# Attention scores on TensorE: from four column strips with a stacked contraction of 97 rows to four row strips of 32, issued pair by pair

## What is computed

```python
N, S, D = x.shape                       # 4, 2048, 512
q = (x @ Wq.T).reshape(N, S, H, hd).transpose(0, 2, 1, 3)    # H = 16, hd = 32
k = (x @ Wk.T).reshape(N, S, H, hd).transpose(0, 2, 1, 3)
v = (x @ Wv.T).reshape(N, S, H, hd).transpose(0, 2, 1, 3)
energy = jnp.einsum('nhqd,nhkd->nhqk', q, k)
attn = jax.nn.softmax(energy / jnp.sqrt(jnp.float32(hd)), axis=3)
out = jnp.einsum('nhql,nhld->nhqd', attn, v)
...
x = _layernorm(x + _L0_attn_ref(x, L0_attn_Wq, L0_attn_Wk, L0_attn_Wv), axis=-1)
x = _layernorm(x + _L0_ffn_ref(x, L0_ffn_weights, L0_ffn_scale, L0_ffn_bias), axis=-1)
```

## Time and profile before

| | us |
|---|---|
| median of 3 runs | 2922.89 (2919.54 to 2924.14) |
| span of the profiled execution | 2917.2 |
| PE busy | 2785.6 (95%) |
| PE weight loads busy | 1423.5 (49%) |
| DVE busy | 2319.8 (80%) |
| ACT busy | 2300.0 (79%) |
| attention, from the first to the last exponential | 610.4 to 2623 |

### The profile page before, as it was taken

The page is one execution under the profiler, slowest core; times in us unless marked ns, Lnnn a source line. Parts: engine busy times, 40 slices in busy tenths (PEclk is TensorE's granted clock), DMA queues, the critical chain, the costliest instruction groups (busy, mean ns, idle before and its releaser), DMA issues.

```text
span 2917.2 us, 79173 instructions
## 1 busy us (share of the span) xinstructions
PE 2785.6 (95%) x29276; PEld 1423.5 (49%) x29276; DVE 2319.8 (80%) x2050; ACT 2300.0 (79%) x2789; POOL 343.1 (12%) x342
## 2 busy tenths in 40 slices
PE   8999999979999999999999999999999999997998
PEld 7888888833333333333333333344343333335887
DVE  4334343469898898989889899898989989897998
ACT  3333333379999999999999999999999999894665
POOL 0000000010000000000000000000000000004665
PEclk9999999989999999999999999999999999998999
DMA  5544445556675766767576675767667576655553
GB/s 190 182 179 173 173 173 180 182 134 144 143 160 117 166 130 140 154 138 153 119 168 128 141 164 123 160 121 162 137 142 167 117 161 134 132 122 182 187 206 130
DMA packets 223563, 445.69 MB, mean 153 GB/s; under 512 B 15442, under 2 KB 130130, under 8 KB 198868
## 3 DMA queue, kind: packets, MB, share of 16 engines
q0 software_dynamic: 27504, 200.29, 35.6%
q1 hardware_dynamic: 186596, 224.71, 24.7%
q10 hardware_dynamic: 9216, 16.78, 1.5%
HBM read 123.47 MB, written 117.96 MB: 83 GB/s over the span
## 4 chain that ended last, share of the span: by engine, by line
PE 73%; issue 4%; ACT 2%; DVE 1%; POOL 0%; ACTq 0%; DMA 0%; SPq 0%; DVEq 0%; POOLq 0%
PE banks L637 33%; PE banks L666 30%; PE banks L1008 6%; PE banks L683 2%; ACT probs L764 1%; PE banks L997 1%; PE banks L990 1%; PE banks L1004 1%; ACT L764 0%; POOL score_rows L587 0%; PE banks L991 0%; DVE partial L821 0%; ACT y L1026 0%; DVE stats L1071 0%; DVE score_rows L773 0%
## 5 line engine op out<-in xcount | busy, mean ns | idle before, releaser
L764 ACT ACTIVATE probs<-banks 128x1024 f32<-128x1024 f32 x2048 | 1891.9, 1149 | 99.6 <-PE banks L637 95.3
L637 PE MATMUL banks<-score_rows 97*32 97x512 f16 x16384 | 1186.8, 384 | 90.1 <-issue 65.8
L666 PE MATMUL banks<-probs,v_keys 128*32 128x512 f32 x8192 | 1094.5, 598 | 3.4 <-issue 3.1
L637 PEld LDWEIGHTS banks<-score_rows 97*32 97x32 f16 x16384 | 431.6, 95 | 1076.1 <-ACT probs L764 578.0
L821 DVE TENSOR_TENSOR partial<-partial,probs 128x2048 f32<-128x2048 f32 x384 | 879.7, 2291 | 50.0 <-ACT probs L764 37.7
L818 DVE TENSOR_TENSOR partial<-probs 128x2048 f32<-128x2048 f32 x192 | 440.2, 2293 | 78.6 <-ACT probs L764 74.0
L606 POOL DMA_DIRECT2D total<-partial x191 | 164.9, 863 | 1847.8 <-DVE partial L821 865.5
L666 PEld LDWEIGHTS banks<-probs,v_keys 128*32 128x32 f32 x8192 | 287.3, 112 | 181.3 <-issue 9.5
L821 DVE TENSOR_TENSOR total<-total,probs 128x2048 f32<-128x2048 f32 x128 | 292.7, 2287 | 2.6
L348 DVE TENSOR_TENSOR qk_lo<-banks,qk_hi 128x512 f16<-128x512 f32 x128 | 88.5, 692 | 240.8 <-ACT qk_hi L292 240.8
L292 ACT ACTIVATE qk_hi<-banks 128x512 f16<-128x512 f32 x128 | 76.4, 597 | 234.2 <-PE banks L246 234.2
(11 more groups left out here) (94 smaller groups left out, 2164.1 us busy)
## 6 DMA issues: line engine op xcount, KB each, us to landing
total<-partial POOLq DMA_DIRECT2D x191, 1024.0 KB, 8.2
x_in<-in_L_attn_x SPq DMA_DIRECT2D x17, 1024.0 KB, 7.3
scratch_q_raw<-qk_raw SPq DMA_DIRECT2D x16, 1024.0 KB, 5.5
scratch_k_raw<-qk_raw SPq DMA_DIRECT2D x16, 1024.0 KB, 5.6
scratch_v<-v_out SPq DMA_DIRECT2D x16, 1024.0 KB, 5.0
score_rows<-scratch_q_hi SPq DMA_DIRECT2D x128, 128.0 KB, 6.4
score_rows<-scratch_k_hi SPq DMA_DIRECT2D x128, 128.0 KB, 3.8
v_keys<-scratch_v SPq DMA_DIRECT2D x64, 256.0 KB, 6.9
```

The source lines that it names most:

```text
L637: last = nc.tensor.matmul(scores_of(unit)[part, i, :], k_rows[:, h, keys], q_rows[:, h, qb * BLK:(qb + 1) * BLK], start=True, stop=True)
L666: last = nc.tensor.matmul(banks[rows, out_bank(qb), :], v_keys[:, kt, rows], probs[:, kt % P_RING, h, :], start=(kt == 0), stop=(kt == KT ...
L764: nc.scalar.activation(probs[:, kt % P_RING, heads, :], scores_of(qb * UNITS + u), ACT.Exp, scale=SCALE / GAIN ** 2).then_inc(a_prob, 1)
```

## The change

The three products become three matmuls that accumulate in PSUM. The high and low parts of q and k now lie in 128 rows, 32 for each of the four heads. A matmul (L628 of the changed kernel) takes one head's 32 rows and makes 128 keys by 512 queries; the four heads use the four row strips of the array. A tile needs 12 such matmuls. The uniform shift moves from the 97th row into the bias operand of the exponential, so POOL's memset and DVE's L773 go, and ACT waits for `a_shift` once. Two DMAs load a block of q or k, not three.

The order on PE is split. Heads 0 and 1 are half 0, heads 2 and 3 half 1; (h,t) below means the two matmuls of half h with term t. `fast_scores` waits for the slot of half 1 and issues (0,1), (1,0), (0,2), (1,1); then comes `values` of the tile two before; then `fast_opening` of the next tile, which waits for that tile's half 0 slot and issues its (0,0); then `fast_closing`, (1,2) of the present tile. Half 0 is complete with (0,2), half 1 with (1,2).

```diff
-        def fast_scores(it, qb, kt):
...
-            for half in range(2):
-                unit = qb * UNITS + 2 * kt + half
-                pe.wait_ge(a_prob, it * ITEM_UNITS + slot_before(unit) + 1 + SLOTS)
-                for i in range(2):
-                    h = 2 * half + i
-                    for c in range(G):
...
-                        last = nc.tensor.matmul(scores_of(unit)[part, i, :], k_rows[:, h, keys],
-                                                q_rows[:, h, qb * BLK:(qb + 1) * BLK], start=True, stop=True)
-                last.then_inc(a_score, 1)
+        def product(qb, kt, half, term):
+            unit = qb * UNITS + 2 * kt + half
+            k_part, q_part = terms[term]
...
+            for i in range(2):
+                rows = slice(HD * (2 * half + i), HD * (2 * half + i) + HD)
+                last = nc.tensor.matmul(scores_of(unit)[:, i, :], k_part[rows, keys], q_part[rows, cols],
+                                        start=(term == 0), stop=(term == len(terms) - 1))
+            return last
+        def fast_opening(it, qb, kt):
...
+            unit = qb * UNITS + 2 * kt
+            pe.wait_ge(a_prob, it * ITEM_UNITS + slot_before(unit) + 1 + SLOTS)
+            product(qb, kt, 0, 0)
+        def fast_scores(it, qb, kt):
+            unit = qb * UNITS + 2 * kt + 1
+            pe.wait_ge(a_prob, it * ITEM_UNITS + slot_before(unit) + 1 + SLOTS)
+            product(qb, kt, 0, 1)
+            product(qb, kt, 1, 0)
+            product(qb, kt, 0, 2).then_inc(a_score, 1)
+            product(qb, kt, 1, 1)
+        def fast_closing(qb, kt):
+            product(qb, kt, 1, 2).then_inc(a_score, 1)
...
+                now = later(it, qb, kt, LAG)
+                following = later(it, qb, kt, LAG + 1)
+                if now and fast:
+                    fast_scores(*now)
...
                 values(it, qb, kt)
+                if following and fast:
+                    fast_opening(*following)
+                if now and fast:
+                    fast_closing(*now[1:])
                 if kt == DEN_TILE and qb > 0:
                     denominators(it, qb - 1)
...
-                                         scale=SCALE / GAIN ** 2).then_inc(a_prob, 1)
+                                         scale=SCALE / GAIN ** 2, bias=shift[:]).then_inc(a_prob, 1)
...
-        nc.gpsimd.memset(k_rows[3 * HD:KROWS], K_SHIFT).then_inc(a_const, 1)
-        pool.wait_ge(a_const, 1)
...
-        dve.wait_ge(a_const, 1)
-        nc.vector.tensor_scalar(q_rows[3 * HD:KROWS], k_rows[3 * HD:KROWS], 0.0, shift[3 * HD:KROWS], ALU.mult, ALU.add).then_inc(a_shift, 1)
```

More of the change, by code:

```diff
@@ L387, in sem @@
         return ctx.enter_context(nc.semaphore(name))
[L389 to L393, removed]
+    rows16 = sb("score_rows", [P, 4, S], FP16)
+    q_hi, q_lo, k_hi, k_lo = (rows16[:, i] for i in range(4))
+    terms = ((k_hi, q_hi), (k_hi, q_lo), (k_lo, q_hi))
+    q_exact = sb("q_exact", [HD + 1, G, BLK], FP32)
+    k_exact = rows16[:].bitcast(FP32)[0:HD + 1]
     v_keys = sb("v_keys", [P, KT, P], FP32)
@@ L434, in attend @@
     m_ones = sem("m_ones")
+    m_zero = sem("m_zero")
     m_q = sem("m_q")
@@ L593, in _ @@
                                 pattern=[[-1, P]], channel_multiplier=1).then_inc(m_id, 1)
-        pool.wait_ge(a_const, 2)
-        nc.gpsimd.memset(first[1][:], 0.0).then_inc(a_const, 4)
+        pool.wait_ge(a_const, 1)
+        nc.gpsimd.memset(first[1][:], 0.0).then_inc(a_const, 1)
         pool.sem_inc(m_max, 2)
@@ L685, in denominators, with later @@
             last.then_inc(a_den, 1)
-        def steps(scores, it, qb, tiles):
-            for kt in tiles:
[L690 to L695, removed]
+        def later(it, qb, kt, by):
+            if kt + by < KT:
+                return it, qb, kt + by
+            if qb < QB - 1:
+                return it, qb + 1, kt + by - KT
+            if it is not LAST:
+                return it + 1, 0, kt + by - KT
+            return None
@@ L696, in steps @@
+        def steps(fast, it, qb, tiles):
+            for kt in tiles:
+                now = later(it, qb, kt, LAG)
+                following = later(it, qb, kt, LAG + 1)
+                if now and fast:
+                    fast_scores(*now)
+                elif now:
+                    exact_scores(*now)
                 values(it, qb, kt)
+                if following and fast:
+                    fast_opening(*following)
+                if now and fast:
+                    fast_closing(*now[1:])
@@ L698, in steps, with item @@
                 if kt == DEN_TILE and qb > 0:
                     denominators(it, qb - 1)
-        def item(scores, it):
-            steps(scores, it, 0, range(HEAD, KT))
+        def item(fast, it):
+            steps(fast, it, 0, range(HEAD, KT))
             for qb in range(1, QB):
-                steps(scores, it, qb, range(KT))
+                steps(fast, it, qb, range(KT))
             if it is not LAST:
-                steps(scores, it + 1, 0, range(HEAD))
+                steps(fast, it + 1, 0, range(HEAD))
@@ L708, in item, with all_items @@
             denominators(it, QB - 1)
-        def all_items(scores):
+        def all_items(fast):
+            if fast:
+                fast_opening(0, 0, 0)
             for kt in range(LAG):
-                scores(0, 0, kt)
-            steps(scores, 0, 0, range(HEAD))
+                if fast:
+                    fast_scores(0, 0, kt)
+                    fast_opening(0, 0, kt + 1)
+                    fast_closing(0, kt)
+                else:
+                    exact_scores(0, 0, kt)
+            steps(fast, 0, 0, range(HEAD))
```

43 lines of the change are left out of this document (22 added, 21 removed).

## The result

The change made the kernel slower: 3187.35 us (median of 4 runs, 3185.32 to 3189.58) against 2922.22 us, a ratio of 1.0906 with a 95% interval of 1.0891 to 1.0922. The time lay in the stated range, 7 us from the forecast. How it came about is only partly what the forecast says: ACT's exponentials, the step from PE to ACT and the changes of shape were mis-sized, and the errors cancel.

What follows compares the result with a forecast made beforehand. ACT's pace bounds the kernel before, a loop of waits the changed one: tiles +258 us, denominators +18, stalls -15, start -4, sum +257, so 3180 us; the case's own range 3060 to 3250, the wide one 2985 to 3290.

Steps and rivals of the forecast that it cites:

- Row strips run side by side: PE's scores: four row strips run together as column strips do, so three rounds of 0.22 us a tile replace four.
- the rival of slower rounds: PE's score rounds: row strips not fully side by side; rounds of 0.30 give 3260 us, pairs in turn 3500; 13%.
- The loop through values: Half 1's path from free slot through values to exponential done: 2.93 us over 2.75, so 1.925 us a tile before shape changes.
- Changes of shape: PE alternating row and column strips twice a tile: 0.20 us for both changes, 0.06 for each of two uncovered weight loads.
- the rival of no cost: PE's switches between row and column strips are free, only the longer path remains: about 3005 us (2975 to 3040); 17%.
- The bias operand at 0: ACT's exponential: the added bias operand costs 0, as no more elements pass.
- 0.56 us from the last round to ACT: Step from the start of PE's last score round to ACT's start: 0.56 us, taken from a row showing 0.57.
- The sum for two tiles: Loop of waits over two tiles: 3.85 us plus 0.20 for shape changes and 0.12 for loads, 4.17; one tile 2.085.
- Denominators and stalls: Losses outside the steady tile: 64 denominators at 0.65 us for 0.37, +18 us; PE's stalls and ACT's table load, -15.
- Start: Attention's start: PE's first matmul waits for loads, not POOL and DVE, coming at 603 to 604 for 607.90: -4 us.
- One long and one short tile in turn: Steady stretch: a tile every 2.05 to 2.1 us, long and short alternating, since the loop spans two tiles.
- The rival on the faster side: PE's path isn't the limit, its 0.22 us a tile helps it catch up after denominators and stalls: 2870 us; 7%.

Runs made afterwards that it cites:

- shifted kernels: Kernel before with 32, 64 or 96 one-column matmuls issued once ahead of the first scores: 2948.63, 2966.34 and 2943.33 us.

## Why the prediction was right, point by point

**ACT's pace bounds the kernel before: right.** A longer exponential alone takes the tile to 2.010 us, twice ACT's new pace, and a small matmul more on PE leaves it at 1.834. The changed kernel itself doesn't test this: PE lost a round of 0.22 us and got 0.24 for the changes of shape, 0.22 + 0.22 + 0.32 + 0.45 + 0.55 = 1.76 us a tile for 1.74 (forecast 1.78).

**Row strips run side by side: right.** Rounds of four start 0.22 us apart, so the rival of slower rounds falls, and with it the estimate of 0.29 us worked out from the Trainium skill ("TensorE: Matmul & The Clock Gate", Part 3).

**The loop through values: right as a mechanism.** Alone in the kernel before it costs 0.14 us a tile. Moving the closing product out of it takes the changed kernel's tile from 2.080 to 2.010 us, where ACT's pace takes over, and without the operand from 1.990 to 1.914.

**Changes of shape: right in kind and size.** The forecast took 0.20 for the changes and 0.06 for a load of 128 columns of fp16. The trace has 0.32 into values, 0.45 within, 0.55 out, beyond 0.22, 0.43 and 0.43 that is 0.24 in all, and loads of 0.09 us that cost nothing that can be seen behind half 1's wait. The rule of the Trainium skill ("TensorEngine Tiling (Array Packing)", Key Properties) holds for row against column strips too; 0.24 us is its price for a change there and back in this kernel, and the rival of no cost falls.

**The bias operand at 0: wrong, the step that failed.** The forecast says "no more elements pass; 0". It costs 0.088 us an exponential, from idle and in a row. The kernel before had rows that could have warned: two ACTIVATE groups of 128x512, the copy out of PSUM without pointer operands and the normalisation out of SBUF that has both scale and bias. The page of the changed kernel repeats them with the same mean times, 598 and 809 ns:

```profile
L294 ACT ACTIVATE v_out<-banks 128x512 f32<-128x512 f32 x64 | 38.3, 598 | 125.5 <-PE banks L244 125.5
L1062 ACT ACTIVATE y<-res,offset,rstd 128x512 f32<-128x512 f32 x128 | 97.9, 809 | 10.0 <-DVE offset L1121 3.7
```

0.21 us between them, if all of it is the two operands, is 0.1 for each; function and source differ too, so it is an estimate. The Trainium skill ("ScalarE: Activation LUTs", What ACT_TABLE_LOAD costs) has it too: each pointer operand adds about 93 ns. The measured 88 ns agree. It weighs twice in the loop of two tiles: in half 1's own exponential, and in the next one's pace.

**0.56 us from the last round to ACT: wrong for half 1.** It was read behind a stall where a half 0 exponential started. Half 1's starts 0.44 us after, in all kernels; ACT has two waits fewer before it, which may be why.

**The sum for two tiles**, forecast against measured: 0.05, 0.44, values with both changes and loads 1.18, 0.56, 1.02, 0.92 make 4.17. In the trace, 0.05, 0.22, 0.32, 0.45, 0.55, 0.44, 1.11, 1.005 make 4.15, and two tiles take 4.16. ACT's two terms are 0.18 higher, the step to ACT 0.12 and the changes with their loads 0.08 lower. Had only the bias been right, the forecast would have been 0.09 us a tile higher, near 3270: still under the wide range's 3290, but over the 3250 of the case's own. The nearness of 3180 to 3187 is luck.

**Denominators and stalls: +3 forecast, +23 measured.** The losses go from 135 to 158 us. The denominators were sized well: by the ends of the exponentials around them a block loses 0.36 us before and 0.71 after (forecast 0.37 and 0.65), +22 for 64 blocks where +18 was forecast. The rest, -15 in the forecast, came to +1. The shifted kernels show that it moves by 25 to 52 us with the place of the code, so its sign was not to be had from the trace.

**Start: -4 forecast: right.** The attention's own way to PE's first matmul is 3.7 us shorter; the first exponential comes 5.8 us sooner because the projection ended 2.5 sooner, which no term had.

**One long and one short tile in turn: right.** Most tiles alternate between 2.01 and 2.15 us; the short one is twice ACT's pace of 1.005, the long one has what the loop needs beyond it. In some blocks, as at 1500 us, the two are nearly even (2.07 and 2.09), with the same sum.

**The rival on the faster side** decided at 2.75 us for half 1's way from a free slot. Measured it is 3.14, against a limit that itself rose to 3 x 1.005 = 3.02; without the operand it is 3.05 against 2.75.

## What to carry to other kernels

With few slots between two engines, count the time from "slot free" to "slot free" for each slot, through everything that stands between its wait and its last instruction in program order, and compare it with the slots' number times the pace; the engines' busy shares can't show it. Price every operand that an instruction on the bounding engine gains, from a row of the same engine that has it. When two kernels differ by a per cent and their steady stretches are equal, suspect the place of the code before the change.

## What the runs showed of the hardware that was not expected

- Going from 32-column to 32-row strips and back costs 0.24 us; 128-column fp16 weights for a row strip load in 0.09 us, where the 128-column fp32 ones take 0.19.
- A pointer bias adds 0.088 us to an exponential of 128x1024, alone (1.02 to 1.11) and in a row (0.917 to 1.005).
- 64 to 192 more instructions, executed once ahead of PE's loop, made the time 23 to 46 us longer at the same steady tile; an extra matmul in each of 1024 tiles made the kernel 22 us faster.
- PE's long stalls in the shifted kernels (4.4 to 5.9 us) come where its loop jumps back, once a round, each with a fetch of instructions that starts 2 to 3 us before PE goes on.
